# A masked attention and mixture-of-experts kernel: ScalarE's casts reordered around the first transposed rows, one cast moved to GpSimd, the threshold guesses of batches 2 and 3 moved up by one to two steps

## The reference, cut to what matters

```
# adjacency step, per batch
Q, K = ctx @ Wq.T, ctx @ Wk.T                      # 4 heads of 16
sim  = sum over heads of Q K^T / (sqrt(16) * 4)      # 256 x 256
thr  = the 76th largest value of each row of sim     # k = int(256 * 0.3)
A    = sigmoid(sim) * (sim >= thr);  A = (A + A^T) / 2
x    = x + (1 - g) * layernorm(x) + g * A            # g = sigmoid(gamma_raw)
# experts, per row
xn = layernorm(x)
p  = softmax(xn @ gate_w); the two best experts, their shares renormalised, times alpha
y  = sum over e of comb[e] * (gelu(xn @ fc1_w[e] + fc1_b[e]) @ fc2_w[e] + fc2_b[e])   # 8 experts, 256 -> 256 -> 256
x  = x + y
```

## Time and profile before

| | |
|---|---|
| runs of the kernel before | 135.66, 135.93, 136.01 us, median 135.93 |
| the profiled execution | 135.68 us, its span 133.9 us |
| busy share of the span | TensorE 90%, VectorE 72%, ScalarE 67%, GpSimd 48% |
| TensorE's granted clock, mean | 0.987 of full |

### The profile page before, as it was taken

The page is one execution under the profiler, slowest core; times in us unless marked ns, Lnnn a source line. Parts: engine busy times, 40 slices in busy tenths (PEclk is TensorE's granted clock), DMA queues, the critical chain, the costliest instruction groups (busy, mean ns, idle before and its releaser), DMA issues.

```text
span 133.9 us, 2763 instructions
## 1 busy us (share of the span) xinstructions
PE 120.3 (90%) x904; PEld 110.1 (82%) x904; DVE 96.1 (72%) x399; ACT 89.5 (67%) x213; POOL 64.4 (48%) x65
## 2 busy tenths in 40 slices
PE   6796985289999999999699999996999999999990
PEld 3443753279998999999599999995999999999990
DVE  0068897193799489999987699999787436933472
ACT  3188999959999849866388498645954644446510
POOL 2047658715763974543059535330793335453300
PEclk9999999968999999999999999999999999999999
DMA  2999948995396000002000000020000002000002
GB/s 64 250 389 417 410 164 133 198 197 105 47 149 120 5 0 0 2 5 78 0 2 0 2 5 2 0 78 2 5 0 0 5 0 78 0 0 5 2 0 78
DMA packets 3380, 10.05 MB, mean 75 GB/s; under 512 B 396, under 2 KB 868, under 8 KB 3364
## 3 DMA queue, kind: packets, MB, share of 16 engines
q1 hardware_dynamic: 2500, 6.71, 13.8%
q0 software_dynamic: 864, 3.15, 13.6%
HBM read 8.81 MB, written 1.05 MB: 74 GB/s over the span
## 4 chain that ended last, share of the span: by engine, by line
PE 56%; DVE 21%; ACT 16%; issue 4%; DVEq 0%; ACTq 0%
PE p_y L477 23%; PE p_h L455 22%; DVE acc L1052 5%; ACT w_hi L557 4%; ACT w_lo L559 3%; DVE left L871 3%; ACT h_act L574 2%; DVE above L833 2%; PE p_y L355 2%; PE p_g L339 1%; ACT h_hi L582 1%; DVE picked L1009 1%; PE p_y L339 1%; DVE left L882 1%; PE p_g L403 1%
## 5 line engine op out<-in xcount | busy, mean ns | idle before, releaser
L688 POOL TENSOR_TENSOR h_lo<-h_act,h_hi 128x512 fp32r<-128x512 f32 x31 | 40.5, 1309 | 48.1 <-ACT h_hi L582 33.3
L574 ACT ACTIVATE h_act<-p_h,small_sb 128x256 f32<-128x256 f32 x64 | 26.7, 469 | 19.3 <-PE p_h L455 18.4
L455 PE MATMUL p_h<-xt_hi,w_hi 128*128 128x256 f32 x128 | 33.7, 286 | 2.9 <-ACT xt_hi L566 2.7
L455 PE MATMUL p_h<-xt_hi,w_lo 128*128 128x256 f32 x128 | 33.3, 282 | 0.0
L1052 DVE SCALAR_TENSOR_TENSOR acc<-p_y,comb,acc 128x256 f32<-128x256 f32 x55 | 24.0, 476 | 11.0 <-PE p_y L477 10.2
L477 PE MATMUL p_y<-w_hi,h_hi 128*128 128x256 f32 x126 | 26.1, 288 | 2.5 <-DVE acc L1052 2.5
L455 PEld LDWEIGHTS p_h<-xt_hi,w_hi 128*128 128x128 f32 x128 | 24.6, 193 | 3.4 <-issue 3.3
L455 PE MATMUL p_h<-xt_lo,w_hi 128*128 128x256 f32 x128 | 26.0, 284 | 0.0
L477 PE MATMUL p_y<-w_hi,h_lo 128*128 128x256 f32 x126 | 25.0, 280 | 0.0
L477 PE MATMUL p_y<-w_lo,h_hi 128*128 128x256 f32 x126 | 25.0, 280 | 0.0
L455 PEld LDWEIGHTS p_h<-xt_hi,w_lo 128*128 128x128 f32 x128 | 24.7, 193 | 0.0
(11 more groups left out here) (141 smaller groups left out, 184.6 us busy)
## 6 DMA issues: line engine op xcount, KB each, us to landing
w_sb<-w SPq DMA_DIRECT2D x8, 512.0 KB, 7.9
w_lo<-w POOLq DMA_DIRECT2D x6, 512.0 KB, 5.7
x_sb<-x SPq DMA_DIRECT2D x1, 768.0 KB, 8.2
out<-acc SPq DMA_DIRECT2D x3, 256.0 KB, 2.5
x_sb<-x SPq DMA_DIRECT2D x1, 256.0 KB, 4.1
out<-acc SPq DMA_DIRECT2D x2, 128.0 KB, 2.0
attn_sb<-attn SPq DMA_DIRECT2D x1, 192.0 KB, 4.7
small_sb<-small SPq DMA_DIRECT2D x1, 97.5 KB, 4.3
```

The source lines that it names most:

```text
L455: last = nc.tensor.matmul(dst, w_[:, e, 0, k, c * P:(c + 1) * P], v[:, b % 2, k, :], start=n == 0, stop=n == len(trio) - 1)
L574: last = nc.scalar.activation(h_act[:, s % 2, c], tiled(p_h[s % 2])[:, c, :], ACT.Gelu, bias=b1_sb[:, e, c:c + 1])
L688: nc.gpsimd.tensor_tensor(h_lo[:, s % (LAG + 1)], h_act[:, s % 2], h_hi[:, s % (LAG + 1)], ALU.subtract).then_inc(h_lo_ready, 1)
```

## The change

It does four things. (1) `POOL_HI` goes from 2 to 3: GpSimd casts `w_hi` of expert 2 as well; the rest of expert 2 is still the negative from ScalarE and the adding DMA, so the `2` in `up` and `down` is now written out. (2) `weight_hi(e)` on ScalarE is split into the cast `weight_hi(e)` and the negative `weight_neg(e)`, and these are put in another order: of experts 2 to 7, five pieces stand ahead of `xt_hi_of(0)` where eight did, one between the second sign pass and step 0, and five in steps 0 to 2 where four did in steps 0 and 1. The cast of `b2` goes from ahead of the steps to step 3. (3) GpSimd's adding DMAs follow: that of expert 2 and 3 each one place earlier, that of 5, 6 and 7 behind `hidden_lo` of steps 0, 1 and 2. (4) For batches 2 and 3 `spread_of` goes from e = 5 to 4 on ScalarE, `guesses` from e = 7 to 5 and `middle_guess` from e = 0 to the 7 before on VectorE, the sign passes from 7 and 0 to 6 and 7 on ScalarE, `better_guess` to `drop_above` from e = 1 to 0, and `drop_eight` from 2 to 1.

```diff
-POOL_HI = 2
+POOL_HI = 3
...
@@ scalar
             def weight_hi(e):
                 act.wait_ge(w_in[e], 16)
                 nc.scalar.activation(w_hi[:, e], w_sb[:, e], ACT.Copy).then_inc(w_hi_ready, 1)
-                act.wait_ge(w_hi_ready, e - POOL_HI + 1)
+
+            def weight_neg(e):
+                if e < POOL_HI:
+                    act.wait_ge(w_hi_early, e + 1)
+                else:
+                    act.wait_ge(w_hi_ready, e - POOL_HI + 1)
                 nc.scalar.activation(w_lo[:, e], w_hi[:, e], ACT.Copy, scale=-1.0).then_inc(w_neg_ready, 1)
...
             sigmoid(0)
-            weight_hi(POOL_HI)
+            weight_neg(2)
+            weight_hi(3)
+            weight_neg(3)
             for b in range(1, BATCHES):
                 sim_copy(b)
             nc.scalar.activation(gate_parts[:, :, 0], gate_sb, ACT.Copy).then_inc(gate_hi_ready, 1)
-            weight_hi(POOL_HI + 1)
             spread_of(1)
-            act.wait_ge(b2_in, 16)
-            nc.scalar.activation(b2_hi[:], b2_sb[:], ACT.Copy).then_inc(b2_hi_ready, 1)
-            weight_hi(POOL_HI + 2)
-            weight_hi(POOL_HI + 3)
+            weight_hi(4)
+            weight_neg(4)
             signs_of(1)
             xt_hi_of(0)
             signs_again_of(1)
+            weight_hi(5)
             for s in range(STEPS):
...
-                if e == 0 and more and b:
-                    signs_again_of(b + 1)
...
-                if POOL_HI + 4 + s < EXPERTS:
-                    weight_hi(POOL_HI + 4 + s)
+                if s < 3:
+                    weight_neg(5 + s)
+                if s < 2:
+                    weight_hi(6 + s)
+                if s == 3:
+                    act.wait_ge(b2_in, 16)
+                    nc.scalar.activation(b2_hi[:], b2_sb[:], ACT.Copy).then_inc(b2_hi_ready, 1)
...
-                if e == 5 and b + 2 < BATCHES:
+                if e == 4 and b + 2 < BATCHES:
                     spread_of(b + 2)
+                if e == 6 and b + 2 < BATCHES:
+                    signs_of(b + 2)
                 if e == 7 and b + 2 < BATCHES:
-                    signs_of(b + 2)
+                    signs_again_of(b + 2)
@@ gpsimd
             weight_hi(1)
+            weight_hi(2)
             base(0)
             weight_lo(1, 0)
+            weight_rest(2)
             pool.wait_ge(gate_hi_ready, 1)
...
-            weight_rest(2)
+            weight_rest(3)
             pool.wait_ge(masked, TILES)
             weight_lo(0, 1)
-            weight_rest(3)
             rstd(veps2, rstd2, 0, ln2_veps, ln2_rstd)
             weight_rest(4)
             pool.wait_ge(xn_ready, TILES)
             weight_lo(1, 1)
-            weight_rest(5)
...
-                    weight_rest(6)
-                if s == 1:
-                    weight_rest(7)
+                if s < 3:
+                    weight_rest(5 + s)
@@ vector
-                if more and b and e == 0:
-                    for t in range(TILES):
-                        middle_guess(nxt, t)
-                if more and e == (1 if b else 0):
+                if more and e == 0:
                     for t in range(TILES):
                         better_guess(nxt, t)
...
+                if more and e == 1:
                     drop_eight(0)
-                if b and b < BATCHES and e == 2:
+                if 0 < b < BATCHES and e == 2:
+                    top2(b)
                     combine(b)
-                if more and b and e == 2:
-                    drop_eight(0)
...
+                if e == 5 and nxt + 1 < BATCHES:
+                    guesses(nxt + 1)
...
+                if e == 7 and nxt + 1 < BATCHES:
+                    for t in range(TILES):
+                        middle_guess(nxt + 1, t)
                 if more and e == 7:
                     xt_lo_of(nxt)
-                if e == EXPERTS - 1 and nxt + 1 < BATCHES:
-                    guesses(nxt + 1)
+                if e == 7 and nxt + 1 < BATCHES:
                     ln1(nxt + 1)
```

More of the change, by code:

```diff
@@ L438, in up @@
                 if b == 0:
-                    if e < POOL_HI:
+                    if e < 2:
                         pe.wait_ge(w_lo_ready[e][0], 1)
@@ L461, in down @@
                 b, e = divmod(s, EXPERTS)
-                if b == 0 and e < POOL_HI:
+                if b == 0 and e < 2:
                     pe.wait_ge(w_lo_ready[e][1], 1)
@@ L661, in weight_rest @@
             def weight_rest(e):
-                pool.wait_ge(w_neg_ready, e - POOL_HI + 1)
+                pool.wait_ge(w_neg_ready, e - 1)
                 nc.gpsimd.dma_start(w_lo[:, e], w[:, e].bitcast(F32R), accum_op=ALU.add).then_inc(w_rest_in[e], 16)
@@ L1114, in _ @@
                     drop_above(nxt)
-                if b < BATCHES and e == (2 if b else 0):
-                    top2(b)
+                if s == 0:
+                    top2(0)
                 if more and e == 1:
```

## The result

The changed kernel takes **130.33 us** (median of 4 runs, 130.10 to 130.67) against 135.8 for the kernel before on the same chip: ratio 0.960, 95% interval 0.957 to 0.964. Forecast were 130.4 in a range of 129.6 to 132.3. The profiled execution took 130.10 us (span 128.3) against 135.68 (span 133.9), so there are 5.58 us to account for.

What follows compares the result with a forecast made beforehand. TensorE, busy 90% of the span, was taken as the bound, apart from its waits. 135.68 less 2.7 (opening) and 2.8 (two stalls) gave 130.2, put at a median of 130.4 us; range 129.6 to 132.3.

Steps and rivals of the forecast that it cites:

- the opening: From the start to `up(5)`: fewer pieces of ScalarE work ahead of `xt_hi` bring `up(5)` from 41.87 to 39.2, gain 2.7 us.
- the threshold: Batches 2 and 3: earlier threshold work shortens TensorE's stalls ahead of `down(10)` and `down(18)` by 1.4 each, gain 2.8 us.
- the possible gain for `xn`: Opening, GpSimd's DMA issue no longer ahead of `rstd`: could bring `xn` forward by 0 to 0.4 us, taken as 0.
- The low clock drops out of this sum: Opening: the 3 us at low clock lay inside a stretch that TensorE had caught up on by `up(5)`.
- GpSimd's cast, costed at nothing: Opening: GpSimd's new cast of 1.03 us follows that of expert 1, while `base(0)` waits for VectorE anyway; cost 0.
- The 0.65 from `guesses` and `middle_guess`: VectorE, batches 2 and 3: moving these two to earlier steps makes `add_expert(8)` come 0.65 us earlier.
- The 1.05 of the collision: `drop_above`'s second operation took 1.47 us instead of 0.42 beside GpSimd's `hidden_lo`; running earlier, it would win back 1.05.
- my bounds of 0 to 0.7: What `drop_above`, moved earlier, loses beside GpSimd's small `rstd`: between 0 and the 0.7 us of a `rstd`.
- What the prediction worked out from the rule for `rstd`: `rstd`, starting first, costs `drop_above` its whole 0.7; the stall keeps 0.2 and the sum is 0.2 to 0.3 us higher.
- The collision stays: Rival, chance 0.15: `drop_above` still waits for a `hidden_lo`; each stall keeps 0.6 to 1.2, giving 131.6 to 132.8 us.
- The clock falls again: Rival, chance 0.11: a low-clock stretch of 3 us falls behind `up(5)`; half is lost, 1.5 us, giving 131.9.
- The ramp gains nothing beyond the clock: Rival, chance 0.08: something else holds ScalarE in the opening; half of the 2.7 us gone gives 131.8.
- Slower: Rival, chance 0.02: `up(5)` waits for expert 5's later adding DMA; at 16 us for that DMA the time is 137.7.

## Why the prediction was right, and where not

The total came out at 130.33 for 130.4. That it lies so near is luck: the opening gave 0.6 more than its term and the threshold 0.5 less. One reason was wrong as well.

**The opening, forecast 2.7, measured 3.27.** Each step came as worked out, and a little sooner. `xt_hi` did have to wait for the transposes. These came 0.35 sooner, because the possible gain for `xn` that I had set at 0 was there. GpSimd before, and then after:

```profile
20.96 1.20 POOL L663 DMA_DIRECT2D w_lo<-w  x1
21.84 1.07 POOL L655 TENSOR_TENSOR rstd<-veps,neg_half 128x2 f32<-128x2 f32 x1
...
21.82 0.71 POOL L665 TENSOR_TENSOR rstd<-veps,neg_half 128x2 f32<-128x2 f32 x1 [0.32 <-DVE veps L766]
```

Before, GpSimd was at the issue of a DMA until 22.16, and `rstd` ended at 22.91; now it waits for VectorE's variance and ends at 22.53, 0.38 sooner. The 1.07 against 0.71 is no faster `rstd`: its record begins 0.32 before the issue ends. `gelu(0)` to `gelu(3)` took 11.45 us for 11.68 forecast. Together this is 0.58 of `gelu(3)` (37.65 for 38.23), and `up(5)` followed it as forecast. TensorE idled less ahead of `up(5)` than the 2.5 forecast: pieces of 0.44 and 0.96.

**"The low clock drops out of this sum" was wrong as a reason.** TensorE had not caught up by `up(5)`: the warming matmuls alone bring `up(5)` forward by 0.85 us, since ScalarE's `gelu(0)` waited for a slow `up(0)`. The sum was not hurt by it, since it took `gelu(0)` from where ScalarE would be and so contained the end of that wait. But of the 3.3 us some 0.9 us could have been had with the old order of casts, and the idle time of 1.59 ahead of `gelu(0)`, which was in the rows, was the sign of it.

**GpSimd's cast, costed at nothing: right.** It stands back to back with that of expert 1, and `base(0)` started at 14.57 as before:

```profile
11.49 2.02 POOL L669 CAST w_hi<-w_sb 128x1024 fp32r<-128x1024 f32 x2
...
14.57 1.09 POOL L684 TENSOR_SCALAR x_sb<-x_sb,mul,add 128x256 f32<-128x256 f32 x2 [1.07 <-DVE add L791]
```

A third cast there is hidden as well (130.32). Putting the second back costs 1.0. The adding DMAs, costed at nothing, never show among TensorE's waits.

**The threshold, forecast 2.8, measured 2.31.** The forecast took `add_expert(8)` 1.0 to 1.7 us earlier; it comes 0.91 earlier against `up(12)`. Two steps of it failed:

- The 0.65 from `guesses` and `middle_guess` was counted as a term of its own. Alone it is worth next to nothing (132.39 against 132.51): in batch 1 the moved guesses delay what follows them, in batch 2 VectorE turns the gain into a wait for TensorE. It is worth something only because `drop_above` and what leads to it moved up as well, so that VectorE has work in that wait.
- The 1.05 of the collision was counted as won once `drop_above` got clear. In batch 2, 0.26 of it stayed at `drop_above`. This is not the `rstd` that my bounds of 0 to 0.7 were for, but the `hidden_lo` itself, which I had placed just ahead. Another 0.85 went to the cast in `top2`; in batch 1 only 0.35 came back. I had seen that what follows would come earlier and might meet `hidden_lo(10)`, but watched `picked`, and missed the cast that stands a few small operations ahead of it. And taking the collision away without a change of order gives 0.1 to 0.2 per batch behind the opening (131.95, 135.22).

VectorE's rows add up to the measured gain. The stretch from `acc` + `p_s` to `add_expert` has no wait for another engine in either kernel, and `middle_guess` has left it:

| | batch 1 | batch 2 |
|---|---|---|
| stretch before | 12.92 (52.79 to 65.71) | 12.85 (79.02 to 91.87) |
| stretch after | 11.36 (49.90 to 61.26) | 12.13 (74.17 to 86.30) |
| shorter by | 1.56 | 0.72 |
| by its parts | 0.84 + 1.05 - 0.35 = 1.54 | 0.78 + 1.05 - 0.26 - 0.85 = 0.72 |
| its start, against `up(12)` or `up(20)` | 0.65 later | 0.20 earlier |
| `add_expert` earlier by | 0.91 | 0.92 |

The parts are `middle_guess` and the two collisions. So in batch 1 some 0.7 of the gain is collision and 0.2 order; in batch 2 the collision gave nothing (-0.06), and all of it is order.

The Trainium skill (SBUF — State Buffer, section "Who interferes with whom") also says that a VectorE copy or cast, in a mode that uses both port pairs, and a GpSimd operation exclude each other for a whole instruction. The 1.02 and 1.05 against 0.17 agree with this, for a cast of four columns; that the cast ran in such a mode no trace shows. Had I held each VectorE operation that follows against it, the cast would have been on the list. What the prediction worked out from the rule for `rstd` did not occur: where a `rstd` started first and no `hidden_lo` ran any more (52.83, 0.69), `drop_above` kept its 0.41.

**The rivals.** "The collision stays" came true in part: it moved, and each stall kept 0.27, under the 0.6 to 1.2 forecast for it. (Its price, 131.6 to 132.8, has the 0.1 that the forecast leaves per stall in it twice; the rows give 131.4 to 132.6.) "The clock falls again" did not: 1.00 from 22 us to the end. "The ramp gains nothing beyond the clock" did not: the opening gives 3.3 and the clock 0.9 of it. "Slower" by a late DMA did not: no wait of `up(5)` for a DMA, it waited 0.96 for `gelu(3)`.

**The signs** given: `xt_hi` 23.73 for 24.1, `gelu(3)` 37.65 for 38.2, `up(5)` 38.60 for 39.2, full clock, each wait for `acc` behind `up(5)` under 0.3 (0.27, 0.26), `drop_above` at most 0.67 for 0.7. Only `up(13)` to `up(21)` missed, with 25.02 us for 24.7. TensorE's wait of 0.26 in it is the cast's; with cast and indices gone the stretch took 24.66, with the cast only moved 24.93.

## What to carry to other kernels

- Where two engines exclude each other and both repeat every few microseconds, don't count a collision as won when one operation gets clear of it: list the operations behind it, slide them by what is won, and see which one falls beside the next. An operation of 0.17 us counts there as much as a long one.
- In a written order, work that is moved off a stretch helps only if what comes next there has its data; look for the wait that it will turn into, and move work up into that.
- An idle time of the engine that a slowed engine feeds says that the low clock is on the path. Ask who waited at the slow stretch, not whether the slow engine caught up later.

## What the runs showed of the hardware

- A VectorE cast of four elements per partition takes 0.17 us, and up to 1.05 beside one GpSimd subtraction of 128 x 512 of 1.29 us: six times its length. It ends 0.01 to 0.04 us behind the subtraction in all 15 places where the two meet.
- A VectorE operation with two inputs of 128 x 256 (`drop_above`, 0.41 alone) ends 0.28 to 0.29 us behind such a subtraction in all 18 places, in twelve traces, where its record overlaps one, and takes up to 1.48 us. Beside a `rstd` alone it kept 0.41 to 0.42. The count, with one input of 128 x 256, kept its 0.47 beside the subtraction (76.53).
- The stretch at half clock is not of one length. Behind the same wait of 2.7 us it was 3 us in one profiled execution and 6.4 us in another, and the kernel before alone shows two groups of mean granted clock, 0.3 us apart in time (135.87 and 135.60). 20 more warming matmuls kept it away. What sets its length is open.
- GpSimd's `rstd` on 128 x 2 values takes about 0.7 us. The records of 1.07 and 1.01 begin 0.32 and 0.35 before the operation ahead has ended (a DMA issue, and a subtraction that itself follows one), so a record's length alone can mislead: compare the ends. Those of 0.87 stand between a `hidden_lo` and a `drop_above` that waits for it.
